# A ring of three slots instead of four for the granules of the first half, and a fifth granule of the second half loaded by quarters

## What is computed

```python
x = x + _L0_conv_ref(_gn(x), L0_conv_weight)       # depthwise 5x5 convolution (16 of 25 taps), padding 2
x = x + _L1_conv_ref(_gn(x), L1_conv_rota_matrix)  # einsum('hvc,bchw->bvhw', R, x): one 128x128 matrix per row h
```

## Time and profile before

| | |
|---|---|
| median of 3 runs | 433.54 us (432.03 to 433.54) |
| profiled execution, its own time | 432.79 us |
| its span, first to last instruction | 431.0 us |
| TensorE busy | 405.3 us, 94% |
| VectorE busy | 362.9 us, 84% |
| ScalarE / GpSimd busy | 265.1 / 243.4 us |
| moved by DMA | 139.83 MB, mean 324 GB/s |

### The profile page before, as it was taken

One profiled execution on the slowest core, in us unless ns is written; L12 is line 12 of the kernel. 1 busy time (PEld: TensorE's weight loads), 2 busy tenths in 40 slices (PEclk: granted clock), 3 DMA queues, 4 the chain that ended last, 5 costly groups with the idle time before them and its releaser, 6 DMA issues.

```text
span 431.0 us, 8607 instructions
## 1 busy us (share of the span) xinstructions
PE 405.3 (94%) x3110; PEld 200.0 (46%) x3110; DVE 362.9 (84%) x691; ACT 265.1 (62%) x513; POOL 243.4 (56%) x312
## 2 busy tenths in 40 slices
PE   7899999999999999999999999999999979999930
PEld 2345555555555555544544444454544433444410
DVE  4899999999999999888998998899976885878730
ACT  2476675667566756787666667776676426777700
POOL 7598675766576756677655557764541153544400
PEclk9999999999999999999999999999999998999975
DMA  7836587789977797977999999999998899999998
GB/s 294 366 69 227 197 280 293 256 315 367 366 237 234 234 340 248 354 259 271 307 375 375 346 394 288 383 331 385 388 383 316 298 379 398 399 412 427 425 426 336
DMA packets 36811, 139.83 MB, mean 324 GB/s; under 512 B 7328, under 2 KB 7456, under 8 KB 24224
## 3 DMA queue, kind: packets, MB, share of 16 engines
q1 hardware_dynamic: 16912, 107.28, 65.9%
q10 hardware_dynamic: 19856, 31.99, 20.9%
HBM read 72.14 MB, written 67.12 MB: 323 GB/s over the span
## 4 chain that ended last, share of the span: by engine, by line
PE 89%; DMA 2%; POOL 2%; issue 1%; DVE 1%; ACT 1%; ACTq 0%; SPq 0%; POOLq 0%
PE ps L738 63%; PE ps L773 25%; POOL area L442 2%; DMA area<-in_x_dram 1%; DMA norm<-affine 1%; PE ps L748 1%; ACT gn L537 1%; PE ps L756 0%; ACTq L259 0%; DVE stats L605 0%; POOL area L456 0%; DVE area L647 0%; SPq L303 0%; ACT std L509 0%; DVE affine L625 0%
## 5 line engine op out<-in xcount | busy, mean ns | idle before, releaser
L738 PE MATMUL ps<-area 64*64 64x496 f32 (+2 forms) x2560 | 281.6, 586 | 1.9 <-POOL area L442 1.9
L738 PEld LDWEIGHTS ps<-area 64*64 64x64 f32 x2560 | 140.2, 133 | 98.1 <-issue 86.5
L442 POOL TENSOR_TENSOR area<-mask,area 128x325 f32<-128x325 f32 x128 | 132.5, 1058 | 44.0 <-PE ps L738 32.8
L516 ACT ACTIVATE area<-area,affine 128x256 f32<-128x256 f32 x192 | 98.1, 592 | 34.6 <-DVE affine L627 32.7
L773 PE MATMUL ps<-gn,rot 128*128 128x512 f32 x256 | 116.1, 606 | 3.2 <-ACT gn L537 2.9
L529 ACT ACTIVATE area<-ps 64x512 f32<-64x512 f32 x128 | 75.9, 593 | 30.7 <-PE ps L738 28.1
L605 DVE BATCH_NORM_STATS2 stats<-area 128x6 f32<-128x512 f32 x128 | 80.6, 690 | 3.9 <-DMA area<-in_x_dram 3.9
L614 DVE BATCH_NORM_STATS2 stats<-area 128x6 f32<-128x512 f32 x128 | 81.0, 695 | 1.1
L456 POOL TENSOR_SCALAR area<-area,affine 128x256 f32<-128x256 f32 x62 | 46.3, 755 | 63.1 <-DVE affine L627 62.9
L773 PEld LDWEIGHTS ps<-gn,rot 128*128 128x128 f32 x256 | 47.8, 192 | 68.5 <-issue 59.9
L647 DVE TENSOR_TENSOR tin<-ps,tin 128x512 f32<-128x512 f32 x68 | 46.8, 691 | 15.0 <-PE ps L773 14.9
(11 more groups left out here) (26 smaller groups left out, 109.8 us busy)
## 6 DMA issues: line engine op xcount, KB each, us to landing
area<-in_x_dram SPq DMA_DIRECT2D x31, 1024.0 KB, 6.7
x_scratch<-area ACTq DMA_DIRECT2D x29, 1024.0 KB, 8.4
out_dram<-tin SPq DMA_DIRECT2D x17, 1024.0 KB, 9.8
tin<-x_scratch SPq DMA_DIRECT2D x15, 1024.0 KB, 11.7
area<-x_scratch SPq DMA_DIRECT2D x10, 1024.0 KB, 12.0
out_dram<-area SPq DMA_DIRECT2D x10, 1024.0 KB, 22.1
rot<-in_rota_dram SPq DMA_DIRECT2D x4, 1024.0 KB, 8.8
kept<-x_scratch SPq DMA_DIRECT2D x16, 256.0 KB, 9.8
```

The lines of the kernel that those rows point to most:

```text
L442: last = nc.gpsimd.tensor_tensor(taps[k % TRING][:, c * KW:(c + 1) * KW].rearrange("p d (b r) -> p d b r", r=TAPS), mask[:].rearrange("p d ...
L516: last = nc.scalar.activation(normed[k % GRING][:, :, j], x_of(k)[:, :, j], ACT.Identity, scale=affine[:, k % AFFINES, 0, 0, j:j + 1], bia ...
L738: last = nc.tensor.matmul(ps[half, bank + c].rearrange("p (j w) -> p j w", j=J)[:, :, outs], taps[k % TRING][rows, (2 * pair + c) * KW + d ...
```

## The change

The ring has three slots instead of four. `kept` has five instead of four; the fifth belongs to granule 20, which before took over ring slot 1. Granule 20's first three quarters are now issued in the loop, at s = 26, 30 and 31, and no longer after it. In the loop the ring load is issued last, behind the quarters and the loads of granules 13 to 15. Granule 21 (in a buffer of the convolution) is then the only one that is loaded by quarters into such a buffer without waiting for a store.

```diff
-DRING = 4
+DRING = 3
-FRONT = 4
+FRONT = 5
...
-        tin += [own[1], granule_on(at_x[5]), own[2], granule_on(at_n[0]), granule_on(at_n[1]), granule_on(at_t),
-                granule_on(at_t + TILE), granule_on(at_x[0]), own[3], granule_on(at_x[1]), own[0], granule_on(at_x[2])]
+        tin += [granule_on(at_x[5]), own[1], granule_on(at_n[0]), granule_on(at_n[1]), granule_on(at_t),
+                granule_on(at_t + TILE), granule_on(at_x[0]), own[2], granule_on(at_x[1]), own[0], granule_on(at_x[2])]
...
-            return 16 * QUARTERS if UNITS <= n < UNITS + FRONT + 3 else 16
+            return 16 * QUARTERS if UNITS <= n < UNITS + FRONT + 2 else 16
...
+                n = s - 29 + KEPT
+                if KEPT <= n < UNITS:
+                    await_stores(sp, s - 3)
+                    sp.wait_ge(stats_ready, measured(s - 3 + LAG))
+                    load_granule(sp, n)
+
+                for r, steps in ((0, (22, 23, 24, 25, 26)), (1, (26, 27, 28, 29, 30)), (2, (30, 30, 31, 31, 31))):
+                    for n in range(FRONT):
+                        if steps[n] == s:
+                            await_stores(sp, PER_HALF + (r + 1) * PER_QUARTER - 1)
+                            load_quarter(sp, UNITS + n, r)
+
                 n = s - START + 1
                 if 2 <= n < KEPT:
                     if n >= DRING:
                         sp.wait_ge(out_stored[n - DRING], 16)
                     load_granule(sp, n)
 
-                n = s - 29 + KEPT
-                if KEPT <= n < UNITS:
-                    await_stores(sp, s - 3)
-                    sp.wait_ge(stats_ready, measured(s - 3 + LAG))
-                    load_granule(sp, n)
-
-                for r, steps in ((0, (22, 23, 24, 25)), (1, (26, 27, 28, 29)), (2, (30, 30, 31, 31))):
-                    for n in range(FRONT):
-                        if steps[n] == s:
-                            await_stores(sp, PER_HALF + (r + 1) * PER_QUARTER - 1)
-                            load_quarter(sp, UNITS + n, r)
-
-            sp.wait_ge(out_stored[9], 16)
-            for r in range(QUARTERS - 1):
-                load_quarter(sp, 20, r)
             await_stores(sp, STEPS_ALL - 3)
```

## The result

The changed kernel takes 435.99 us (median of 10 runs, 432.96 to 438.02) against 432.95 us for the kernel before (10 runs, 431.73 to 433.54). The ratio is 1.0071 with a 95% interval of 1.0049 to 1.0093: slower by 0.7% and clear of the noise. The median is inside the range that was given, 431.0 to 438.0, and just outside the 431.2 to 435.5 that the forecast of no change covers. The spread has grown too, from 1.8 to 5.1 us.

The account below looks back on a forecast made before the run. TensorE sets 12.5 us steps, DMA close behind; a transfer backlog about 16 us deep ends the kernel. Convolution steps 0, end of convolution -0.8, small stalls +0.3: 431.0 to 430.5 us span, 433.0 on the median's footing; range 431.0 to 438.0.

Parts of the forecast that it names:

- the forecast of no change: Whole kernel: 433.0 us on the median's footing, ring lateness hidden, covering 431.2 to 435.5 us; chance 0.62.
- What ends the kernel: Tail: a backlog of transfers about 16 us deep, moved by when the last convolution step is stored and bytes left.
- Granule 20's quarters: -0.8, between 0 and -1.9.: End of the convolution: quarters moved to steps 26, 30 and 31 leave less queued, gaining 0.8 us, between 0 and 1.9.
- my second rival: End of the convolution: the last step's store lands up to 2.8 us sooner, giving 430.7 us; chance 0.14.
- First ring loads: the store 9.1 to 11.1 us, the load 7.3.: Ring steps: load waits for the same step's store, taken as 10.1 us; arrives 1.9 us late at GpSimd, 1.2 at ScalarE.
- Free time: 4.8 us at GpSimd, 3.6 at ScalarE, and TensorE stalls behind an eviction.: Ring steps: this idle time absorbs the ring loads' lateness, so TensorE loses 0 us unless ScalarE's lateness reaches 3.6 us.
- "No drift, or at most 0.2 us a step": Ring steps: DMA pauses are filled, so lateness grows at most 2 us over ten steps, which ScalarE still holds.
- the 0 for the convolution steps in the sum: Convolution steps: the ring of three slots adds 0 us to the span.
- 0.3 to 2.2 us of unfilled pause against 0.44 us free: DMA in each ring step: pause between store and load left unfilled, giving no drift to 1.8 us of growing lateness.
- ScalarE's stores land sooner, and T comes every 12.5 us.: Ring steps: SyncE's pause speeds ScalarE's stores, so T, the ring store's issue, comes evenly and x loads are not late.
- The first rival: Ring steps: the ring becomes the bound, drift past 0.25 us a step stalls TensorE, 439 to 440 us; chance 0.24.

Follow-up runs that it names:

- e4b: The kernel before, four slots and old order, with only granule 20's first three quarters moved to the end of step 31; 431.16 us, ratio 0.9967.
- e2: The kernel before with three ring slots, granule 20 loaded where it was, and the ring load issued last in its step; 436.85 us, ratio 1.0117.
- e1: The kernel before with three ring slots alone, granule 20 in the freed slot, loaded where it was before; 441.22 us, ratio 1.0207.
- e3: The changed kernel with the ring load at its old place, ahead of the quarters and of granules 13 to 15; 441.14 us, ratio 1.0198.
- e9: The changed kernel with all fifteen early quarters of granules 16 to 20 issued in step 31; 439.24 us, ratio 1.0130.
- e7: The changed kernel with granule 20's first quarter moved from step 26 to step 31; 436.02 us, ratio 1.0076.
- e10: The changed kernel with the ring store right behind the x load and ahead of the wait for the sum; 436.48 us, ratio 1.0075.
- e5: The changed kernel with the ring store at the head of its step, ahead of the x load; 431.58 us, ratio 0.9982.

## Why the prediction was wrong, point by point

- *What ends the kernel* was read rightly: the delay of the last step's store went through to the end, and what DMA had less to do there came back.
- *Granule 20's quarters: -0.8, between 0 and -1.9.* Right in kind and about half in size: e4b has them alone and gains 1.4 us. In the ring of three the gain is not told well: 2.0 us from e2 to the changed kernel by the ratios, 0.4 from e1 to e3. The last step's store took 4.3 us in e4b where it had taken 7.2, much as my second rival had it, and the kernel gained half of that. Whether granule 21's quarters had held that store, or granule 20's, no run has parted.
- *First ring loads: the store 9.1 to 11.1 us, the load 7.3.* In steps 22 to 25 the stores landed in 9.1 to 10.2 us, as priced, and the first five ring loads (granules 3 to 7) in 5.0 to 6.3, sooner than priced; those of granules 8 to 10 then took 7.4 to 8.0 us, and the stores that they waited for 11.1 to 12.7. The lateness of 1.9 us that I gave every granule was too much for granules 3 to 5, which had none, and far too little for granules 8 to 10.
- *Free time: 4.8 us at GpSimd, 3.6 at ScalarE, and TensorE stalls behind an eviction.* Right. The granules with waits of 0.8 and 1.6 us at GpSimd cost nothing, and the stalls come where ScalarE waits 4.5 to 5.4 us.
- *"No drift, or at most 0.2 us a step"*, and with it the 0 for the convolution steps in the sum, is the step that failed. Three slots in the order of the change cost 4.6 us (e2 against the kernel before), which granule 20's quarters then made up in part. I had worked out 0.3 to 2.2 us of unfilled pause against 0.44 us free, and took the low end on two rows of transfers that had DMA nearly to themselves. Those rows do not stand for a queue in which the next `x` load and the next store are behind the ring load. The measured spacing of ring loads is 13.25 and 14.0 us in the changed kernel between 232 and 273, and 12.6 to 14.5 in e9, thus 0.1 to 2 us of drift a step: the bounds were good, the choice between them was not. The 2.0 us of fixed cost that the prediction takes from the Trainium skill ("DMA: Bandwidth & Descriptors", "Anatomy of one DMA") are given there for transfers issued by GpSimd; those here are issued by SyncE and ScalarE. The sum did not rest on them.
- *ScalarE's stores land sooner, and T comes every 12.5 us.* Sooner, but not soon enough. The stores issued from 209.86 to 247.35 took 11.0 to 13.2 us, and where one took over 12.5 or so the `x` load and T behind it were late: T came 0.4 us late at 235.25 and 1.1 at 248.48. At 259.86 such a store took 15.3 us, and the next `x` load had to wait for it until 275.18.
- The first rival is what happened, with its place and, as far as the rows tell, its threshold: up to 2.0 us of waiting at ScalarE (granule 6 in e7) cost nothing, 4.5 us and more did, and 3.6 lies between. It was priced at 6 us for a drift of 0.9 from the first granule on; in the profiled execution, one of the faster ones, the stalls were 3.1 us, as the lateness began only with granule 6. The profiles of e7 and e10, kernels of the same time, have 5.6 and 5.9 us. What it left out is that lateness feeds itself through the queue's order.
- That the ring load was put behind the quarters I counted as nothing. With three slots it is worth 4.4 us (e1 against e2). The loss of only 0.7% is luck in so far as this and granule 20's quarters made up for two thirds of the 9 us that the ring alone costs.

What is left open: whether e5 gains more by the store's lead of 3 to 4 us or by having no `x` load in front of it.

## What to carry to other kernels

A ring slot taken away turns a wait that was a step old into one on a transfer just issued. Add the two latencies and also ask what the queue holds in between: if the next round's transfers stand behind the late one, lateness grows from round to round, and a margin that held for three rounds here did not hold for ten. Issue the transfer that others wait for as soon as its data are there, and put whatever waits last in its round, behind all that does not. And before a buffer is given up for an earlier load, look whether an existing one comes free in time: here it did, and gave the whole gain alone.

## What the runs showed of the hardware

A 1 MB store of ScalarE's queue took 5.3 us to land beside a nearly empty SyncE queue in the kernel before, and 14.7 us one step earlier beside a full one. In the changed kernel, where SyncE waits some 9 us in each step and issues nothing, the stores issued from 209.86 to 259.86 took 11.6, 12.5, 13.2, 11.0 and 15.3 us: the pause helped them less than I had thought.

The kernels with late ring loads also repeated less well. Between the fastest and the slowest run lie 5.1 us in the changed kernel and 6.0 in e10, but 1.8 with four slots and 2.5 in e5, which has three slots and hardly a late load (ten to twelve runs each).
